# One-hots of a graph kernel written two slots at a time by tensor operations, with the order of its first stage changed

## The reference

```
m   = segment_sum(xt[src], dst) * Binv[:, None]      # layer 1, twice: mean by destination, and back
out = segment_sum(m[dst], src) * Dinv[:, None] + b
red = segment_sum(h[src] + relvectors[rel], dst)     # layer 2, then a GRU cell
out = segment_sum(norm[:, None] * (h @ W.T)[src], dst)   # layer 3, then a layer norm
```

## Time and profile before

| | us |
|---|---|
| Median of 3 runs | 1391.84 (1390.71 to 1392.54) |
| The profiled execution's own time | 1394.6 |
| Its span in the profile | 1392.2 |
| TensorE (PE) busy | 1238.9 |
| VectorE (DVE) busy | 820.4 |
| ScalarE (ACT) busy | 443.2 |
| GpSimd (POOL) busy | 200.1 |

### The profile page before, as it was taken

The page is one execution under the profiler, slowest core; times in us unless marked ns, Lnnn a source line. Parts: engine busy times, 40 slices in busy tenths (PEclk is TensorE's granted clock), DMA queues, the critical chain, the costliest instruction groups (busy, mean ns, idle before and its releaser), DMA issues.

```text
span 1392.2 us, 23709 instructions
## 1 busy us (share of the span) xinstructions
PE 1238.9 (89%) x9435; PEld 956.7 (69%) x9435; DVE 820.4 (59%) x2318; ACT 443.2 (32%) x943; POOL 200.1 (14%) x365
## 2 busy tenths in 40 slices
PE   1359999998899999999999999999999999999930
PEld 1235556555799998666788888677777777888830
DVE  3999999998455564433245452344353555544566
ACT  1645654321766673111111211222222222122200
POOL 5450101011100000000011110000000011111163
PEclk9999999999999999999999999999999999999965
DMA  4200000000411111100034431011111011111124
GB/s 146 80 20 1 1 1 1 1 1 1 143 55 58 51 50 58 48 1 1 31 132 162 143 131 62 23 35 35 35 34 35 31 38 33 34 39 39 36 76 121
DMA packets 44355, 70.49 MB, mean 51 GB/s; under 512 B 6726, under 2 KB 28581, under 8 KB 44240
## 3 DMA queue, kind: packets, MB, share of 16 engines
q1 hardware_dynamic: 36428, 53.67, 11.4%
q10 hardware_dynamic: 4132, 10.63, 2.2%
q0 software_dynamic: 3680, 4.63, 1.3%
HBM read 39.04 MB, written 29.85 MB: 49 GB/s over the span
## 4 chain that ended last, share of the span: by engine, by line
PE 68%; DVE 24%; POOL 4%; ACT 2%; issue 2%; DMA 1%; POOLq 0%; DVEq 0%; ACTq 0%
PE ps L448 36%; PE ps L728 10%; DVE big L1617 5%; DVE whh L1617 5%; PE ps L695 3%; DVE Wg L1606 3%; PE ps L789 3%; PE ps L791 3%; DVE W L1606 3%; PE ps L684 2%; DVE wih L1608 2%; PE ps L1759 2%; POOL adj L671 2%; PE ps L832 2%; PE ps L815 2%
## 5 line engine op out<-in xcount | busy, mean ns | idle before, releaser
L448 PE MATMUL ps<-big,pairB 125*128 125x250 fp8e4 (+1 forms) x2600 | 304.3, 268 | 0.6 <-DVE big L1121 0.6
L448 PEld LDWEIGHTS ps<-big,pairB 125*128 125x128 f16 x2600 | 239.6, 98 | 30.4 <-issue 2.8
L1759 PE MATMUL ps<-pairA,adj 125*125 125x512 f16 x625 | 222.9, 414 | 0.0
L643 POOL TENSOR_TENSOR st<-st,mhalf 125x1 f32<-125x1 f32 x100 | 59.4, 594 | 880.8 <-DVE st L1198 880.8
L448 PE MATMUL ps<-adj,pairB 125*128 125x250 fp8e4 (+1 forms) x1300 | 146.0, 267 | 1.8 <-DVE pairB L1256 1.8
L448 PE MATMUL ps<-adj,pairA 125*128 125x250 fp8e4 (+1 forms) x1300 | 139.2, 267 | 0.0
L1695 ACT ACTIVATE adj<-ps 125x450 fp8e4<-125x450 f32 (+7 forms) x197 | 98.0, 507 | 129.3 <-PE ps L1784 128.9
L448 PEld LDWEIGHTS ps<-adj,pairB 125*128 125x128 f16 x1300 | 123.3, 98 | 20.0 <-DVE pairB L1256 2.0
L728 PE MATMUL ps<-pairA,adj 125*125 125x512 f16 x625 | 135.2, 379 | 0.0
L448 PEld LDWEIGHTS ps<-adj,pairA 125*128 125x128 f16 x1300 | 121.0, 98 | 19.2 <-issue 7.7
L728 PEld LDWEIGHTS ps<-pairA,adj 125*125 125x125 fp8e4 x625 | 85.5, 137 | 49.1
(11 more groups left out here) (238 smaller groups left out, 1822.4 us busy)
## 6 DMA issues: line engine op xcount, KB each, us to landing
t_adjTp<-big SPq DMA_DIRECT2D x25, 400.0 KB, 2.4
big<-t_adjTp ACTq DMA_DIRECT2D x25, 400.0 KB, 4.1
t_xh<-work SPq DMA_DIRECT2D x13, 256.0 KB
t_z<-big SPq DMA_DIRECT2D x25, 128.9 KB
pairB<-in_x SPq DMA_DIRECT2D x5, 640.0 KB, 11.2
t_h0p<-pairB SPq DMA_DIRECT2D x5, 640.0 KB, 2.9
work<-t_xh SPq DMA_DIRECT2D x25, 128.0 KB, 2.2
xin<-t_xh SPq DMA_DIRECT2D x25, 128.0 KB, 2.2
```

What stands on the lines that cost most here:

```text
L448: last = pe.matmul(out, src[:, j, FEAT * part + 128 * c:FEAT * part + 128 * (c + 1)], rhs(j, p), start=(j + part == 0 and not begun), stop ...
L643: g.tensor_tensor(st[:, 9:10], st[:, 8:9], k.mhalf[:, 0:1], ALU.pow).then_inc(S[rstd], 1)
L1759: last = pe.matmul(k.ps[0:P, 6 + t % 2, :], k.adj[:, j, PITCH * i:PITCH * i + P], k.pairA[:, j, :], start=(j == 0), stop=(j == TILES - 1))
```

## The change

The one-hots of a bulk are now written by four tensor_tensor operations. `match` compares, for eight slots at once, a row of counted words with the slot's word, where a word is four fp8 columns; a product with the slot's 32-bit `key_value` then writes `hot_keys` for all eight slots as 32-bit words. All compared operands lie so that the innermost run is stored side by side: two slots (`match`, `hot_lo`) or eight slots (`hot_rel`) are interleaved in memory. TensorE therefore reads the columns of `hot_lo` 4 bytes apart, and those of `hot_rel`, weights and moving side, 16 bytes apart; before, both were contiguous. `halves` with five operations becomes `words_of` with twelve. `hot_lo` and `hot_rel` have three buffers instead of two (`DEPTH`), and TensorE waits once for eight slots instead of once for four.

Windows are at most 10 nodes wide instead of 13, which makes 615 slots. Slots have 112,375 columns of `hot_keys` together, and had 118,500. `SUM_FROM` is 88 instead of 56, so 600 products stand behind slots 88 to 614. From slot 88 on there are 527 slots with 92,625 columns; 73 of them have a second product behind them.

The order of the first stage changes on all engines. On GpSimd the rows of the first table are followed by the first near gather; the rest of the table is cut in two and goes later. On VectorE `chunks`, `starts` and `keys` of the groups 1 to 4, `magnitudes` and `scales` move behind the first bulks, and `words_of(0, 1)` directly behind the first keys. `h(n)` on ScalarE copies five tiles by one instruction. A first-turn product waits for its own tile of the low half only, where it waited for all 25.

```diff
-WIDEST = 13
-KW, KWI = 328, 164
+WIDEST = 10
+KW, KWI = 252, 128
+DEPTH = 3
-SUM_FROM = 56
+SUM_FROM = 88
+        self.iota_pairs = self.big[:, at + 512:at + 512 + 4 * KWI].bitcast(F16).rearrange("p (n b) -> p n b", b=2)
+        self.iota_rel = self.big[:, at + 512 + 4 * KWI:at + 512 + 4 * KWI + 2 * RELS * BULK].bitcast(F16).rearrange("p (n u) -> p n u", u=BULK)
+        self.hot_lo = [flat[2][:, :], flat[3][:, :], gates[:, 0:BULK * 128]]
@@ gpsimd @@
-        table(RUN_SPLIT, SLOTS)
-        iota(k.iota_keys, [[1, KWI]], 0, 0)
+        iota(k.iota_pairs, [[1, KWI], [0, 2]], 0, 0)
+        iota(k.iota_rel, [[1, RELS], [0, BULK]], 0, 0)
         g.memset(k.ho_all[:, :], 0.0).then_inc(iotas, 1)
         gather_near(0)
+        table(RUN_SPLIT, RUN_THIRD)
+        gather(0)
         root(0)
-        gather_near(1)
-        gather_near(2)
-        gather(0)
-        for n in range(3, GROUPS):
+        root(1)
+        table(RUN_THIRD, SLOTS)
+        for n in range(1, GROUPS):
             gather_near(n)
+        root(2)
         for n in range(1, GROUPS):
             gather(n)
-        for n in range(1, BATCH):
+        for n in range(3, BATCH):
             root(n)
@@ vector @@
         def bulk(m):
-            if m >= 2:
-                dve.wait_ge(used, BULK * (m - 1))
+            if m >= DEPTH:
+                dve.wait_ge(used, BULK * (m - DEPTH + 1))
...
-            for u in range(BULK):
...
-                last = v.tensor_scalar(k.hot_keys[m % RING][:, u, 0:2 * n].bitcast(U16), k.iota_keys[:, 0:n],
-                                       k.key_half[:, s:s + 1], k.key_byte[:, s:s + 1], ALU.is_equal, ALU.mult)
+            v.tensor_tensor(same, k.iota_pairs[:, 0:n, :].unsqueeze(1).to_broadcast([128, BULK // 2, n, 2]),
+                            word.to_broadcast([128, BULK // 2, n, 2]), ALU.is_equal).then_inc(hot, 1)
+            v.tensor_tensor(k.hot_lo[m % DEPTH].rearrange("p (a n b) -> p a n b", n=128, b=2),
+                            k.iota_pairs[:, 0:128, :].unsqueeze(1).to_broadcast(rows), low.to_broadcast(rows), ALU.is_equal)
+            v.tensor_tensor(k.hot_rel[m % DEPTH].rearrange("p (k n u) -> p k n u", k=8, u=BULK)[:, 0:2, :, :],
+                            k.iota_rel.unsqueeze(1).to_broadcast([128, 2, RELS, BULK]),
+                            k.key_low[:, 1:3, part].unsqueeze(2).to_broadcast([128, 2, RELS, BULK]), ALU.is_equal)
+            dve.wait_ge(hot, 2 * m + 1)
+            v.tensor_tensor(k.hot_keys[m % RING][:, :, 0:4 * n].bitcast(U32).rearrange("p (a b) n -> p a b n", b=2),
+                            same.rearrange("p a n b -> p a b n"),
+                            k.key_value[:, part].rearrange("p (a b) -> p a b", b=2).unsqueeze(3).to_broadcast([128, BULK // 2, 2, n]),
+                            ALU.mult).then_inc(hot, 1)
...
         keys(0, 1)
+        dve.wait_ge(iotas, 2)
+        words_of(0, 1)
         for m in range(-(-SLOTS // BULK)):
+            if BULK * m == SLOT:
+                words_of(1, GROUPS)
+            bulk(m)
             if m == 0:
+                chunks(1, GROUPS)
+            if m == 1:
+                moments_of(2)
+                magnitudes()
+                starts(1, GROUPS)
+            if m == 2:
+                moments_of(3)
+                scales()
+            if m == 3:
+                moments_of(4)
+            if m == 8:
                 keys(1, GROUPS)
@@ scalar @@
             for i in range(per * n, per * (n + 1)):
                 s.activation(k.xall[:, i, :], k.xall[:, i, :], ACT.Relu, bias=shift[:, i:i + 1],
                              scale=dev[:, i:i + 1]).then_inc(h_own, 1)
-                act.wait_ge(h_own, i + 1)
-                s.activation(k.pairA[:, i, 0:FEAT], k.xall[:, i, :], ACT.Copy).then_inc(h_ready, 1)
+            act.wait_ge(h_own, per * (n + 1))
+            s.activation(k.pairA[:, part, 0:FEAT], k.xall[:, part, :], ACT.Copy).then_inc(h_ready, per)
@@ tensor @@
-            if s % QUAD == 0:
-                pe.wait_ge(hot, s // QUAD + 1)
+            if s % BULK == 0:
+                pe.wait_ge(hot, 2 * (s // BULK) + 2)
-            low, rel = k.hot_lo[m % 2][:, u, :], k.hot_rel[m % 2][:, u, :]
+            low = k.hot_lo[m % DEPTH].rearrange("p (a n b) -> p a n b", n=128, b=2)[:, u // 2, :, u % 2]
+            rel = k.hot_rel[m % DEPTH].rearrange("p (n u) -> p n u", u=BULK)[:, :, u]
         place(0, 1)
+        turn_keys(0)
         place(1, GROUPS)
```

More of the change, by code:

```diff
@@ L90 @@
 RUN_SPLIT = next(r[0] for r in RUNS if r[0] >= SLOT)
+RUN_THIRD = next(r[0] for r in RUNS if r[0] >= (RUN_SPLIT + SLOTS) // 3)
 PADDED = EDGES + (max(w.slots for w in WINDOWS) + 1) * SLOT
@@ L1577, in scales @@
             dve.wait_ge(bound, 1)
-            own.link(stt(out=absb, in0=k.ps[0:P, 5, 0:FEAT], scalar=16.0, in1=absb, op0=ALU.mult, op1=ALU.add))
+            own.link(stt(out=absb, in0=k.ps[0:P, 7, 0:FEAT], scalar=16.0, in1=absb, op0=ALU.mult, op1=ALU.add))
             own.link(v.tensor_reduce(scratch[:, 0:1], absb, AX.X, ALU.max))
@@ L1588, in scales, with words_of @@
             own.link(v.tensor_tensor(k.gslope[:, :], k.gscale[:, :], k.slope[:, :], ALU.mult))
-        def halves(a, b):
+        key_word = k.work[:, 4 * FEAT:4 * FEAT + GROUPS * SLOT].bitcast(F16)[:, 0:GROUPS * SLOT]
+        def words_of(a, b):
             dve.wait_ge(key_out, b)
             part = slice(SLOT * a, SLOT * b)
-            hi, half, byte = k.key_hi[:, part], k.key_half[:, part], k.key_byte[:, part]
-            own.link(v.tensor_scalar(half, hi, 0.5, -0.25, ALU.mult, ALU.add))
-            own.link(v.tensor_scalar(half, half, 12582912.0, None, ALU.add))
-            own.link(v.tensor_scalar(half, half, -12582912.0, None, ALU.add))
-            own.link(stt(out=byte, in0=half, scalar=-2.0, in1=hi, op0=ALU.mult, op1=ALU.add))
-            own.link(v.tensor_scalar(byte, byte, ODD - EVEN, EVEN, ALU.mult, ALU.add))
+            hi, word, value = k.key_hi[:, part], k.key_word[:, part], k.key_value[:, part]
+            own.link(v.tensor_scalar(value, hi, 0.5, -0.25, ALU.mult, ALU.add))
+            own.link(v.tensor_scalar(value, value, 12582912.0, None, ALU.add))
+            own.link(v.tensor_scalar(value, value, -12582912.0, None, ALU.add))
+            own.link(v.tensor_scalar(word, value, 0.5, -0.25, ALU.mult, ALU.add))
+            own.link(v.tensor_scalar(word, word, 12582912.0, None, ALU.add))
+            own.link(v.tensor_scalar(word, word, -12582912.0, None, ALU.add))
+            own.link(stt(out=hi, in0=value, scalar=-2.0, in1=hi, op0=ALU.mult, op1=ALU.add))
+            own.link(stt(out=value, in0=word, scalar=-2.0, in1=value, op0=ALU.mult, op1=ALU.add))
+            own.link(v.tensor_scalar(hi, hi, float(0x3800 - 0x38), float(0x38), ALU.mult, ALU.add))
+            own.link(v.tensor_scalar(value, value, 65535.0, 1.0, ALU.mult, ALU.add))
+            own.link(v.tensor_tensor(value, value, hi, ALU.mult))
+            own.link(v.tensor_copy(key_word[:, part], word))
@@ L1612, in bulk @@
[L1612 to L1620 removed]
+            n = max((TILES * WINDOWS[SLOT_WINDOW[s]].width + 3) // 4 for s in range(BULK * m, min(BULK * (m + 1), SLOTS)))
@@ new lines, in bulk @@
+            rows = [128, BULK // 2, 128, 2]
+            low = k.key_low[:, 0, part].rearrange("p (a b) -> p a b", b=2).unsqueeze(2)
+            word = key_word[:, part].rearrange("p (a b) -> p a b", b=2).unsqueeze(2)
+            same = k.match[m % 2][:, 0:BULK * n].rearrange("p (a n b) -> p a n b", n=n, b=2)
+            v.tensor_tensor(same, k.iota_pairs[:, 0:n, :].unsqueeze(1).to_broadcast([128, BULK // 2, n, 2]),
+                            word.to_broadcast([128, BULK // 2, n, 2]), ALU.is_equal).then_inc(hot, 1)
@@ L1640, in vector @@
         v.tensor_copy(k.identb[:, :], k.ident)
-        chunks(1, GROUPS)
         v.memset(k.big[96:128, 0:2 * BULK * KW].bitcast(U32), 0)
@@ L1794, in place, with bounds @@
         def place(a, b):
-            pe.wait_ge(tabled, 2 if a == 0 else 3)
+            pe.wait_ge(tabled, 2 if a == 0 else 4)
             for g in range(a, b):
                 for n, row in enumerate((first_node, skipped)):
-                    last = pe.matmul(k.ps[:, 4 if a else 0, 2 * g + n:2 * g + n + 1], row[:, SLOT * g:SLOT * (g + 1)], k.ones[0:1, 0:1],
+                    last = pe.matmul(k.ps[:, 7 if a else 0, 2 * g + n:2 * g + n + 1], row[:, SLOT * g:SLOT * (g + 1)], k.ones[0:1, 0:1],
                                      start=True, stop=True)
             last.then_inc(placed, 1)
+        def bounds():
+            pe.wait_ge(abs_ready, 1)
+            mag = k.work[:, 0:2 * FEAT].rearrange("f (c n) -> f c n", c=KC)
+            for c in range(KC):
+                last = pe.matmul(k.ps[0:P, 7, 0:FEAT], k.ones[:, :], mag[:, c, :], start=(c == 0), stop=(c == KC - 1))
+            last.then_inc(bound, 1)
         place(0, 1)
+        turn_keys(0)
         place(1, GROUPS)
-        pe.wait_ge(abs_ready, 1)
```

(9 more changed lines are left out.)

60 lines of the change are left out of this document (18 added, 42 removed).

## The result

| | us |
|---|---|
| Median of 4 runs before, beside them | 1391.52 (1390.71 to 1392.54) |
| Median of 4 runs after | 1348.97 (1348.26 to 1349.76) |
| Ratio, 95% interval | 0.9694 (0.9677 to 0.9711) |
| Span of the profile after | 1347.4 (before 1392.2) |

The change made the kernel 42.6 us faster; 52.3 were forecast, with 1339.5 as the time. The time lies in the range (1325 to 1366) and at the upper end of the likeliest case's own (1331 to 1349).

What follows compares the result with a forecast made beforehand. VectorE's bulks were taken to bound `build`, then TensorE from slot 88 on. 84 + 205 + 3 + 5.6 = 297.6 us against 349.9, so 1391.8 - 52.3 = 1339.5 us; range 1325 to 1366.

Steps and rivals of the forecast that it cites:

- likeliest case: Whole kernel: the forecast of 1339.5 us, with its own range from 1331 to 1349 and a chance of 0.56.
- The sum: End of `build`: 84 + 205 + 3 + 5.6 = 297.6 us, against 349.9 before.
- The bound: In `build`: VectorE's bulks set the slots' pace before; with the change TensorE becomes the bound from slot 88 on.
- part 1: A bulk of one-hots on VectorE: 1.6 us instead of 3.4.
- The choice of the fast rate: VectorE's compares: taken at 0.84 ns an element rather than 1.1, so a bulk of 1.6 us rather than 2.6.
- rival 3: VectorE's compares stay at 1.1 ns an element: 11 us more in the head, 1350 us in all; chance 0.13.
- `words_of(1, GROUPS)` ... hides there: VectorE behind slot 88: this work, about 6 us, hides in 24 slots of lead, which are 8.7 us.
- Part 2: TensorE from slot 88 to the end of the stage: 205 us, plus 3 for a lower clock, then 5.6 for 25 products.
- Part 3: Head of `build`, up to slot 0: slot 0 starts at 28.5 us, 17 earlier.
- Part 4: Slot 0 to slot 88, on VectorE: sum 54 us, slot 88 at 82.4, with the transposes of the keys 84.
- Rival 4: In the head, GpSimd and VectorE don't hold each other: up to 13 us off, 1327 to 1330 in all; chance 0.12.

Runs made afterwards that it cites:

- one_rate: The changed kernel with all three compares' second operand standing still along the innermost run and contiguous layouts: span 1353.0 us, ratio 0.9734 to the kernel before.
- split_words: The changed kernel with `words_of` called for one group at a time, ahead of bulks 16, 32, 48 and 64: span 1344.1 us, ratio 0.9679 to the kernel before.
- old_head: The changed kernel's bulk in the earlier order up to slot 88 on GpSimd, VectorE and TensorE: span 1349.4 us, ratio 0.9725 to the kernel before.
- dve_low: The changed kernel with GpSimd's 25 low halves made by VectorE as five operations: span 1342.5 us, ratio 0.9659 to the kernel before.
- rel_contig: The changed kernel with `hot_rel` alone laid out contiguously for each slot, as before: span 1350.4 us, ratio 0.9717 to the kernel before.

## Why the prediction was right, and where it was short

The sum was 297.6 for the end of `build`; it came at 306.9. The direction, the bound and the range were right; of the signs, four failed: slot 0 (30.6 for 28), the last products (301.3 for 292 to 298), no wait of TensorE for VectorE behind slot 88 (one of 2.5), and the relation's loads (144 ns for 101). Step by step:

- **The bound, and part 1.** Right. VectorE's bulk was taken at 1.6 and is 1.66; behind slot 88 TensorE is the bound, whether the bulk takes 1.7 (after) or 2.4 to 2.6 us from start to start (one_rate). With the old bulk, VectorE is the bound again. The choice of the fast rate, made without a row that shows it, was worth 7.5 us where rival 3 said 11.
- **Part 1, "`words_of(1, GROUPS)` ... hides there".** This step failed. It compared 6 us with 24 slots of lead, and took the lead as given. VectorE had lost it: it stood 2.2 us for ScalarE's `scale_high` ahead of the call, then spent 6.7 on the call and 1.6 on the bulk. TensorE stood 2.5 us, and its clock fell behind that for 3.4 us: 4.1 together, of which split_words took back 3.2.
- **Part 2, the formula.** The earlier trace rows give 0.06 + 0.03 + 0.24 - 0.052 = 0.278 for a slot without columns, and the text wrote 0.272. Over 527 slots the slip is 3.2 us. The strided load adds 1.1, waits for ScalarE's copy of `CT` 1.3. With the stall, 205 + 3.2 + 1.1 + 4.1 + 1.3 = 214.7 of the 215.1 measured. The 3 us put on for a low clock at slot 88 did not come; they hid as much of the miss.
- **Part 3, slot 0 at 28.5.** It came at 30.6. The first near gather landed at 13.7 instead of 12 and `root(1)` ended at 21.3 instead of 19.4, so the iotas (34, not 31) ended at 27.1 instead of 24.9, and TensorE's 16 products of `place` start there. VectorE's bulk was done at 28.9: the columns of groups 1 to 4 held slot 0. By itself a late slot 0 costs little, as old_head shows; but VectorE too stood 1.8 us for these columns, and that is carried on.
- **Part 4, 55.5 us from slot 0 to the first product.** Measured 86.2 - 30.6 = 55.6, and that it agrees so well is in part luck. VectorE had the one-hots of slot 88 at 83.2, 52.5 us behind slot 0, where the sum has 54; then TensorE and ScalarE took 3.0 more, where 1.6 was put on for the transposes. GpSimd's low halves stretched 17 operations of the bulks by 0.48 each, where the earlier trace rows gave 20 by 0.46; the mechanism was shown by dve_low. Rival 4 falls.
- **`main`.** It was to keep its time, and is 1.8 us shorter; 1.6 of it is the clock of one stretch (below), which no term of the sum foresaw.

Behind `build`, the rest of the span is 1040.5 to 1041.0 us in eight of the profiles (after among them) and 1042.3 to 1042.9 in five and in the kernel before. In all fourteen TensorE waits 2.2 us for ScalarE in `main`, until 18 us behind the start of the last 25 products. In the six long ones the granted clock is lower just behind that wait, and TensorE has lost 1.6 us by it; in the eight short ones it stays at 1.00. The stretch before and after, with the columns of the earlier trace rows:

```profile
361.00:367.00 6.00, 4.88 (x36) 4.10 (x37) 2.44 (x6) 6.00 (x11) 0.00 (x0) 0.72 0.41 129
318.00:324.00 6.00, 4.80 (x53) 4.51 (x54) 3.12 (x7) 6.00 (x11) 0.00 (x0) 1.00 0.48 149
```

So 1.6 of the 44.8 us by which the spans of before and after differ, and 1.6 of rel_contig's 3.0, lie in work that no edit changed. Open: why the clock falls behind this wait in some profiles and not in others, and whether it does so in the other executions of the same kernel. It is where small steps read from the marks and from the medians part by 2 us.
